# A gated cross-attention and FFN block on one Trainium2 core: reloads of the spilled activations issued from ScalarE's queue instead of SyncE's

## The reference, cut to what matters

```python
x = x + tanh(g_xattn) * mha(layernorm(x), ctx, ctx, ...)          # x: (32, 256, 512)
xq   = fake_quant(layernorm(x), clip_x)
gate = xq @ quant(w_gate).T ; up = xq @ quant(w_up).T             # I = 1408
h    = fake_quant(silu(gate) * up, clip_down)                     # ONE scale over all of h
x    = x + tanh(g_ffn) * (h @ quant(w_down).T)
```

## Time and profile before

| what | us |
|---|---|
| median of 3 runs | 1785.08 |
| the profiled execution, its own time | 1786.49 |
| span of the profiled execution | 1784.6 |
| last stage within the span | about 1597.5 to 1784.6 |
| PE busy over the span | 1622.6 (91%) |
| DVE, ACT, POOL busy over the span | 1296.8, 847.0, 549.1 |
| mean granted clock of TensorE | 0.963 of full speed |

### The profile page before, as it was taken

How to read it: one execution, slowest core, us unless ns; L and a number is a source line. 1 busy time by engine, 2 the same in 40 slices (tenths; PEclk the granted TensorE clock), 3 DMA queues, 4 the chain that set the end, 5 groups by cost and what they waited for, 6 DMA issues and landing times.

```text
span 1784.6 us, 33864 instructions
## 1 busy us (share of the span) xinstructions
PE 1622.6 (91%) x11880; PEld 766.5 (43%) x11880; DVE 1296.8 (73%) x2055; ACT 847.0 (47%) x1132; POOL 549.1 (31%) x782
## 2 busy tenths in 40 slices
PE   3849999999999999999999999955899999989888
PEld 2324444444444444444444444422444444434333
DVE  6716777776876777777768767657677878778666
ACT  3224435336335344354353362336677777757440
POOL 6114234235144243242351341212000000006778
PEclk7969999999999999999999999978899999999999
DMA  6658577586596586675775864453055543017996
GB/s 192 166 133 177 143 178 163 148 187 161 141 200 147 157 190 159 172 166 164 180 166 150 181 164 105 112 178 136 32 218 197 196 176 136 24 48 287 421 409 235
DMA packets 275019, 307.58 MB, mean 172 GB/s; under 512 B 152160, under 2 KB 201312, under 8 KB 272352
## 3 DMA queue, kind: packets, MB, share of 16 engines
q1 hardware_dynamic: 274912, 306.00, 61.3%
HBM read 176.17 MB, written 95.94 MB: 152 GB/s over the span
## 4 chain that ended last, share of the span: by engine, by line
PE 54%; issue 25%; DMA 7%; DVE 7%; POOL 3%; SPq 2%; ACT 2%; POOLq 0%; ACTq 0%; DVEq 0%
PE bank L1316 12%; PE bank L1217 12%; PE bank L1219 11%; PE bank L1218 11%; PE spair L1298 5%; DMA x<-out_dram 4%; POOL yh L628 3%; PE spair L1273 2%; DMA stacks<-mT 1%; ACT pr L671 1%; DVE ndev L961 1%; PE bank L1208 1%; DMA hb<-in_L_ffn_w_gate_dram 1%; DVE bst L869 1%; SPq L359 1%
## 5 line engine op out<-in xcount | busy, mean ns | idle before, releaser
L918 DVE TENSOR_REDUCE mx<-spair 128x4 f32<-128x1024 f32 x256 | 301.4, 1219 | 57.5 <-PE spair L1273 56.9
L671 ACT ACTIVATE pr<-spair 128x1024 f32<-128x1024 f32 x256 | 259.5, 1021 | 138.7 <-PE spair L1298 138.7
L896 DVE SCALAR_TENSOR_TENSOR parts<-bank,bqk,parts 128x512 f16<-128x512 f32 x128 | 96.0, 750 | 203.6 <-ACT parts L660 197.9
L1414 PE MATMUL spair<-xqT,wgT 128*128 128x512 bf16 x704 | 182.4, 382 | 1.2 <-ACT xqT L784 1.2
L1414 PE MATMUL spair<-xqT,wuT 128*128 128x512 bf16 x704 | 181.7, 381 | 0.0
L1298 PE MATMUL spair<-stacks 128*128 128x256 f16 x1024 | 154.1, 277 | 18.2 <-ACT pr L671 11.6
L660 ACT ACTIVATE parts<-bank,bqk 128x512 f16<-128x512 f32 x128 | 88.0, 688 | 172.9 <-PE bank L1219 172.9
L1316 PE MATMUL bank<-pr,v 128*32 128x256 f32 x2048 | 140.3, 392 | 29.0 <-DVE o L912 24.1
L767 ACT ACTIVATE sil<-spair,gsc 128x512 f32<-128x512 f32 x176 | 118.2, 680 | 75.2 <-PE spair L1414 75.2
L553 POOL TENSOR_TENSOR nw<-rt 128x4 f32<-128x4 f32 x96 | 21.1, 220 | 419.6 <-DVE rt L864 414.6
L628 POOL TENSOR_TENSOR yh<-yh,x 128x512 f32<-128x512 f32 x64 | 134.7, 2135 | 49.1 <-DMA x<-out_dram 29.9
(11 more groups left out here) (175 smaller groups left out, 3337.9 us busy)
## 6 DMA issues: line engine op xcount, KB each, us to landing
stacks<-qk_spill SPq DMA_DIRECT2D x384, 128.0 KB, 4.3
qk_spill<-parts SPq DMA_DIRECT2D x64, 512.0 KB, 3.1
x<-out_dram SPq DMA_DIRECT2D x32, 1024.0 KB, 10.9
h_spill<-hb SPq DMA_DIRECT2D x10, 2816.0 KB, 9.2
xbuf<-in_x_dram SPq DMA_DIRECT2D x16, 1024.0 KB, 7.1
cbuf<-in_ctx_dram SPq DMA_DIRECT2D x16, 1024.0 KB, 6.4
xres<-in_x_dram SPq DMA_DIRECT2D x16, 1024.0 KB, 5.6
out_dram<-xres SPq DMA_DIRECT2D x16, 1024.0 KB, 4.3
```

Source lines behind the costliest of these rows:

```text
L671: act.activation(pr[:, u % 4, :, :, :].rearrange("p a b q -> p (a b q)"), spair[u % 2][:, :, :].rearrange("p a q -> p (a q)"), ACT.Exp, sc ...
L896: dve.scalar_tensor_tensor(out=parts[:, c, 2 * w + 1, :], in0=pj[(g + 1) % 3][:, :], scalar=bqk[:, w, c:c + 1], in1=parts[:, c, 2 * w, :], ...
L918: dve.tensor_reduce(mx[:, h:h + 2, b, :], spair[u % 2][:, :, :].rearrange("p a (q k) -> p a q k", q=KH), AX_X, ALU.max).then_inc(max_done, 1)
L1414: last = pe.matmul(spair[k % 2][:, s, :], w[:, kc, t * P:t * P + P], xqT[:, par, kc, :], start=(kc == 0), stop=(kc == KC - 1))
```

## The change

`load_h` leaves SyncE's program and goes into ScalarE's, with the same wait, the same source, the same places and the same semaphore. Load 0 is issued behind the rounding of step 1, and load k (k = 1..9) behind the rounding of step k + 2. SyncE keeps the stores of y and the loads of x1, in the same order as before.

```diff
 # SyncE
-            def load_h(k):
-                wait(sp, ht_done, k + 2 if k > 0 else 1)
-                sp.dma_start(RING[k % len(RING)], h_dram[k]).then_inc(h_in[k % len(RING)], 16)
...
             load_res3(group_of[0], 0)
             load_res3(group_of[1], 1)
-            load_h(0)
...
                 if m + 2 < NG:
                     load_res3(group_of[m + 2], m % 2)
-                if m + 1 < NS:
-                    load_h(m + 1)
 # ScalarE
-            for m in range(1, NG):
+            def load_h(k):
+                wait(act, ht_done, k + 2 if k > 0 else 1)
+                act.dma_start(RING[k % len(RING)], h_dram[k]).then_inc(h_in[k % len(RING)], 16)
+
+            h_round(1)
+            load_h(0)
+            for m in range(2, NG):
                 h_round(m)
+                if 3 <= m < NS + 2:
+                    load_h(m - 2)
```

## The result

The changed kernel takes 1797.28 us (median of four runs, 1791.41 to 1801.56) against 1784.79: a ratio of 1.0070, 95% interval 1.0040 to 1.0101, some 12 us slower. Measured twice more it took 1796.45 (1.0058, 1.0045 to 1.0072) and 1796.17 (1.0064, 1.0049 to 1.0080). Forecast was 1789.6.

What follows compares the result with a forecast made beforehand. The last stage was taken as DMA-bound, then PE-bound. All terms cost 0 except h going ahead of stores and x1, +4.5 us: 1786.5 became 1791.0, or 1789.6 on the runs' scale; range 1776 to 1794.

Steps and rivals of the forecast that it cites:

- SyncE's relief: Ten load issues leave SyncE for ScalarE, whose idle time takes them; nobody waits for the time gained: cost 0.
- ScalarE's new wait: Wait for `ht_done` of k + 2 ahead of load k; roundings queued behind it are read much later: cost 0.
- The second rule: Issuing from several engines saves only the issue time; by that alone the sum would be 0.
- stores and x1 stand in another queue than h: Last stage, full DMA engines: h goes first, PE does a step less before the last load lands, +4.5 us.
- the period stays 11.88: Full DMA stretch of the last stage: if h always goes first, steps still come every 11.88 us.
- the 0.95: Sign: DMA share stays near 1 in the middle; below 0.95 something else binds and all is wrong.
- The rival of two loads ahead: Rival D, last stage: two loads of h get ahead instead of one, 9 us lost, 1794; chance 0.10.
- up to 6.85 us later: If h always goes first, y tiles of step 3 start up to 6.85 us later than 1644.07.
- stores landing later than 12.0 us: Sign that the forecast is right: stores of y land later than 12.0 us after issue.
- Load 1 no longer stands behind the first store: Issue timing: load 1's `ht_done` is reached at 1620.8, against its issue at 1625.55 before.
- Load 0 goes from 1606.4 to about 1610: Issue timing: load 0 moves behind the rounding of step 1; DMA share is 0.47 there, so nothing waits.
- Rival A: Last stage: queues share by bytes, half each; period 10.75, gains 8 us, 1777; chance 0.28.

Runs made afterwards that it cites:

- the first profile: Profiled execution from the first measurement of the changed kernel, 1791.41 us; that measurement's median was 1797.28 us.
- the second: Profiled execution of the changed kernel measured again with no edit, 1792.28 us; that measurement's median was 1796.45 us.
- the third: Profiled execution of the changed kernel measured a third time with no edit, 1796.42 us; that measurement's median was 1796.17 us.

## Why the prediction was right and wrong

**Right**: the direction and its reason. Who goes first decides, not bandwidth; h goes first since its packets are 11 times as long (73 packets against 70); the whole of SyncE's relief and of ScalarE's new wait costs nothing (issues of 0.33 to 0.39 us, and VectorE waits for roundings only at the start of the stage, as before). The last load lands 2.4 us earlier (1732.45 + 1.6 against 1736.46), and PE is behind by then: its step 12 starts at 1745.18 + 1.6 against 1739.85.

The second rule cited of the Trainium skill ("DMA: Bandwidth & Descriptors", section "Issuing engines are not separate DMA queues") would have made the sum 0. The runs bear out that a second queue brings no bandwidth (420 GB/s over 1643 to 1655 us, with both in use) and go against taking it to mean that the time stays.

**Wrong, the term of the sum that was mis-sized**: "stores and x1 stand in another queue than h", at +4.5 us. It held that one load gets ahead once, that "the period stays 11.88" and that the engines stay full. The runs show in its place that an x1 that just misses its gap waits for two loads, and the store queued behind it too (20.1 and 21.9 us to landing; before, no transfer of y or x1 took over 14.3), that this comes back two or three times, and that the closed loop then asks for too little: the DMA share falls to 0.88 in 1655 to 1667 us, below the 0.95 that the prediction had named as the sign of something else at work, and the same stretch of the stage moves 387 GB/s instead of 396, 1.0 MB or about half a step's y and x1. The term measured +6.6 us in the first profile (the two stalls of 9.3 and 9.8 us, and the lower clock behind each, against eight steps before that were each 2.4 us over 9.5), +6.0 in the second, +8.6 in the third, whose execution took about as long as the median one, and 11.3 to 12.5 us in the medians. The rival of two loads ahead, at +9 and one chance in ten, named the mechanism that came, but once and not two or three times.

The y tiles of step 3 were to start "up to 6.85 us later"; they start at 1652.77 + 1.6, 10.3 us later. Of what was to show it, stores landing later than 12.0 us failed as a median (6.4) and holds for the ones that stall (21.9 us). The last load was to be in by 1730; it is in at 1732.45 + 1.6.

**"Load 1 no longer stands behind the first store"** was right in time (issued 1619.23 + 1.6, against 1620.8 reckoned) but priced inside the same term; alone it costs 0.5 us within an error of 1.6.

**"Load 0 goes from 1606.4 to about 1610"** was wrong, without effect: it was issued at 1604.83 + 1.6, as before, while the rounding of step 1 (1603.18 to 1608.24) still ran. An issue behind a rounding in ScalarE's program didn't wait for its end.

**Rival A** (equal shares) was sized -8 us and measured -4 with 2 KB packets; the loop was right (10.9 against 10.75), and the slower short packets, +5 us on one queue, are the likely rest.

What stays open: the 2.7 to 5.9 us by which the medians lie above what the longer stage explains. The stage began between 1594 and 1600.5 us in the fourteen profiles of kernels that are alike up to it or nearly so, so a profile's start may account for it, but the runs without a profile show no stage. How often an unprofiled run of the changed kernel stalls is not known either.

## What to carry to other kernels

A second DMA queue adds no bandwidth to full engines; it replaces the order of issue by a share that the packet lengths set, so compare the contiguous runs of the two kinds of transfer with the share that each needs before one of them is moved. Where a long prefetch and short urgent transfers meet on full engines, cut the prefetch and deal it out evenly between the urgent ones, as far as its deadline allows: here that gave 0.5 to 0.6% with the queue and the bytes as they were. A median time to landing can fall while the kernel gets slower; look at the longest.

## What the runs showed of the hardware that was not expected

While both queues had packets under way, their counts were equal within 5% in the stretches shown, at every length tried (22.5 KB, 5632 B, 2 KB and 1 KB against 2 KB). But a transfer that came to engines filled by the other queue got its first packet only some 4 us after its issue (1622.98 to after 1627), and 1 us after it on idle ones. Full engines moved 421, 404, 395 to 400 and 381 GB/s over 1640 to 1720 us with packets of h of these lengths (the 421 and the 395 with one queue). An issue of 2816 packets of 1 KB held ScalarE's queue for up to 17.4 us, one of 128 packets for 0.33 us. And a transfer that lacked less than half of its bytes (0.45 MB of 1.05) when a load with long packets started waited for nearly all of that load: the share acts on remainders as on whole transfers.
